# Moving one-off preparation of an attention and expert kernel ahead of its main loop, two score stacks prepared by transfers

## The chip, the cores and the metric

The kernel runs on one core of a Trainium2 chip. A core has a matrix engine (TensorE, PE in the profile; PEld is its weight load), a vector engine (VectorE, DVE), an activation engine (ScalarE, ACT), a general engine (GpSimd, POOL) and a synchronisation engine (SyncE, SP), which here issues every transfer. Each engine runs its own list of instructions in order, and waits on semaphores for the others. The metric is the time of one execution on the device in microseconds (us).

## The reference, cut to what matters

`x` is (32, 256, 128): 32 sequences of 256 tokens with 128 features. There are 16 heads of width 8 and 8 experts.

```python
def _attn(x, Wq, bq, Wk, bk, Wv, bv, Wo, bo):      # x: (b, s, 128)
    q, k, v = ((x @ W.T + c).reshape(b, s, 16, 8).transpose(0, 2, 1, 3) for W, c in ...)
    scores = jnp.einsum('bhqd,bhkd->bhqk', q, k) / math.sqrt(8)
    scores = jnp.where(causal, scores, -jnp.inf)
    out = jnp.einsum('bhqk,bhkd->bhqd', softmax(scores), v)
    return out.transpose(0, 2, 1, 3).reshape(b, s, 128) @ Wo.T + bo

def _experts(x, gate_w, We):
    top_val, top_idx = jax.lax.top_k(jnp.einsum('btd,ed->bte', x, gate_w), 2)
    y_all = jnp.einsum('btd,edm->btem', x, We)
    return (take(y_all, top_idx) * softmax(top_val)[..., None]).sum(axis=2)

xn = layernorm(x)
return x + _attn(xn, ...) + _experts(xn, ...)
```

## The kernel before

**One sequence is one unit of work, and 34 slots are laid over 32 sequences.** `over_slots` writes slot `s` for every engine. In slot `s` the kernel takes the scores of sequence `s` with queries as rows, only for their maxima (`score_item` on PE, `take_max` on DVE); the scores of sequence `s-1` with keys as rows, exponentials and weighted values (`scoreT_item`, `take_exp`, `values`), which run `LAG` = 4 items behind and so reach into slot `s+1`; the experts of sequence `s-1`; the output of sequence `s-2`; the projections of sequence `s+2` (`PRE`); and the normalisation of sequence `s+3` (`NXT`). A slot has twelve score items, and each engine's share of the other work stands at fixed item numbers `n`.

**The stacks.** The scores need q and k of a head as bf16 triples (high, middle and low part), stacked as rows of one contraction. `qstack` and `kstack` hold, for each of four buffers, 128 partitions by 16 heads by 256 tokens in bf16, that is 8 KB a partition. Rows 0 to 71 (to 79 for q, with zeros) are loaded for each sequence: ACT, DVE and POOL write the three parts (`part1`, `take_rest`, `part2`, `part3`) into `parts`, SP stores them to a DRAM scratch, waits for that, and loads them back in the order of the stack, six transfers a sequence (`stacks`). One or two more rows (from `MAX_ROW` = 72) take the maxima of `mT`, by two small transfers a sequence. Rows 80 to 122 (`MASK_ROW` to `ALL_ROWS`) of q, and 72 to 122 of k, are the same for all sequences: they encode the causal mask. They are made once in `q_steps` and `k_steps` by POOL and copied into the upper 64 partitions of each stack (`fill_stack` on DVE, `fill_keys` on ACT). `vaug` (values padded with zeros and ones) also needs a one-off fill of each of four buffers.

**What sets the order around the change.** Everything is written out by hand. Before slot 0 stands a preamble: input loads, three normalisations, two projections, the fill of three or four stacks. `between` does one-off work behind slots 0 to 3: on DVE `fill_vaug`, the fill of query stacks 2 and 3 and the split of the expert weights into two halves; on ACT the fill of key stacks 2 and 3 and its part of the split. SP's list in slot `s` is: store the output of sequence `s-3`, load the maxima `mT` of sequence `s-1`, load an input, then `stacks` for sequence `s+2`, whose loads wait in the first slots for `dve_stack` and `act_stack`. All transfers are on SP's one queue.

Of the kernel before, what the change touches and what calls it, by code (L numbers as in the profile page):

```python
# [27 lines left out]
ALU = mybir.AluOpType  # L28
# [86 lines left out]
def bass_block(nc, x, wq, wk, bq, bk, wv, bv, wo, bo, gate, we, out):  # L115
    ctx = ExitStack()
    with ctx:
# [12 lines left out]
        def sems(*names):  # L130
# [80 lines left out]
        act_stack, dve_stack, dve_fill, dve_zero, dve_weights, act_weights = sems(  # L211
            "act_stack", "dve_stack", "dve_fill", "dve_zero", "dve_weights", "act_weights")
# [5 lines left out]
        dve_stats, dve_mv, pool_eps, pool_rstd, pool_xn = sems("dve_stats", "dve_mv", "pool_eps", "pool_rstd", "pool_xn")  # L218
# [13 lines left out]
        LOOP0 = 4  # L232
# [4 lines left out]
        def over_slots(slot, between=None):  # L237

            for s in range(NSEQ + 2):
                slot(Seq(0, s), s)  # L240
                if between and s < LOOP0:
                    between(s)
# [14 lines left out]
        def _(sp):  # L257
# [22 lines left out]
            def stacks(pre, s):  # L280
# [17 lines left out]
                rows = scr.rearrange("a (d h) t -> (a d) (h t)", h=H)  # L298
                qs, ks = (st[pre.buf][:].rearrange("p h t -> p (h t)") for st in (qstack, kstack))
                sp.wait_ge(dma_scratch_q, upto(pre, unit=16))  # L300
                for r in range(PARTS):
                    n = PART_ROWS + (ZERO_ROWS if r == PARTS - 1 else 0)
                    sp.dma_start(qs[r * PART_ROWS:r * PART_ROWS + n], rows[0:n]).then_inc(dma_stack[pre.buf], 16)
                sp.wait_ge(dma_scratch_k, upto(pre, per=2, unit=16))
                for r in range(PARTS):
                    turned = PART_ROWS + ZERO_ROWS + r * HD
                    sp.dma_start(ks[r * PART_ROWS:(r + 1) * PART_ROWS],
                                 rows[turned:turned + PART_ROWS]).then_inc(dma_stack[pre.buf], 16)

            def slot(t, s):  # L310
# [8 lines left out]
                if has(s, NB):  # L319
                    new = t + NB  # L320
                    sp.wait_ge(pool_xn, upto(t))
                    sp.wait_ge(pool_xb, upto(t))
                    sp.dma_start(x_sb[new.buf][:], x_t[new.n]).then_inc(dma_x[new.buf], 16)
# [3 lines left out]
            for s in range(-PRE, 0):  # L327
                stacks(Seq(0, s + PRE), s)
            over_slots(slot)
# [5 lines left out]
        def _(pool):  # L335
            g = nc.gpsimd

            def normalise(nxt):
# [3 lines left out]
                pool.wait_ge(pool_eps, upto(nxt))  # L342
                g.tensor_tensor(rstd[:], var_eps[:], minus_half[:], ALU.pow).then_inc(pool_rstd, 1)  # L343
                pool.wait_ge(pool_rstd, upto(nxt))
# [5 lines left out]
                ins.then_inc(pool_xn, 1)  # L350
# [9 lines left out]
            def mask_steps():  # L360
                g.memset(q_steps[:], 0.0).then_inc(pool_const, 1)
                g.memset(k_steps[:], 0.0).then_inc(pool_const, 1)
                pool.wait_ge(pool_const, CONSTS)

                for i in range(STEPS):
                    g.affine_select(out=k_steps[:], in_=k_steps[:], compare_op=ALU.is_gt, fill=B_STEPS[i],
                                    base=1 + i - STEPS * MASK_ROW, pattern=[[-1, P]], channel_multiplier=STEPS).then_inc(pool_steps, 1)
                    pool.wait_ge(pool_steps, 2 * i + 1)
                    g.affine_select(out=q_steps[:], in_=q_steps[:], compare_op=ALU.not_equal, fill=A_STEPS[i],
                                    base=STEPS * MASK_ROW - i, pattern=[[1, P]], channel_multiplier=-STEPS).then_inc(pool_steps, 1)  # L370
                    pool.wait_ge(pool_steps, 2 * i + 2)
                g.affine_select(out=k_steps[:], in_=k_steps[:], compare_op=ALU.is_ge, fill=1.0,
                                base=-MASK_ROW, pattern=[[0, P]], channel_multiplier=1).then_inc(pool_steps, 1)
# [76 lines left out]
            normalise(Seq(0, 0))  # L450
            mask_steps()
            normalise(Seq(0, 1))
            part3(Seq(0, 0))
            normalise(Seq(0, 2))
            part3(Seq(0, 1))
            over_slots(slot)


        @block.scalar
        def _(act):  # L460
# [16 lines left out]
            def take_values(t, s):  # L477
# [4 lines left out]
                if s < NB:  # L482
                    act.wait_ge(dve_fill, 1 + s)
# [77 lines left out]
            def fill_keys(b):  # L561

                a.copy(kstack[b][HALF:P].rearrange("p h (q t) -> p (h q) t", q=QT),  # L563
                       k_steps[HALF:P].unsqueeze(1).to_broadcast([HALF, H * QT, P])).then_inc(act_stack, 1)
# [13 lines left out]
            copy_input(Seq(0, 0))  # L578
            round_input(Seq(0, 0))
            act.wait_ge(ld_bqk, 16 * 2)  # L580
            part1(Seq(0, 0))
            part2(Seq(0, 0))
            copy_input(Seq(0, 1))
            round_input(Seq(0, 1))
            part1(Seq(0, 1))
            part2(Seq(0, 1))
            copy_input(Seq(0, 2))
            round_input(Seq(0, 2))
            act.wait_ge(pool_steps, 2 * STEPS + 1)
            fill_keys(1)  # L590
            over_slots(slot, between)


        @block.vector
        def _(dve):
# [65 lines left out]
            def halve_input(nxt):  # L661
                dve.wait_ge(act_xnT, upto(nxt))
# [14 lines left out]
            def moments(nxt):  # L677
                dve.wait_ge(dve_stats, upto(nxt))
                dve.wait_ge(pool_xn, upto(nxt + (-1)))
# [12 lines left out]
            def slot(t, s):  # L692
                mix, fin = t + (-1), t + (-2)
                for n in range(ITEMS):
# [35 lines left out]
                    if n == 11 and has(s, NXT):  # L730
                        halve_input(t + NXT)
# [7 lines left out]
            def fill_vaug(b):  # L739

                v.memset(vaug[b][:], 0.0).then_inc(dve_zero, 1)
                dve.wait_ge(dve_zero, 2 + b)
                vv = vaug[b][:].rearrange("p q h c -> p (q h c)")
                ins = v.memset(bass.AP(tensor=vv.tensor, offset=vv.offset + HD,
                                       ap=[list(vv.ap[0]), [VGRP * VW, QT * H // VGRP], [VW + OW, VGRP]]), 1.0)
                ins.then_inc(dve_fill, 1)
# [5 lines left out]

            def between(s):
                if s < NB - 1:
                    fill_vaug(s + 1)
                if s < 2:
                    fill_stack(qstack[s + 2], q_steps)
                if s == 0:
                    dve.wait_ge(ld_we, 16)
                    dve.wait_ge(act_weights, 1)  # L760
                    high_half(we_sb[:], w_high[:]).then_inc(dve_weights, 1)
                    dve.wait_ge(dve_weights, 3)
                    low_half(we_sb[:], w_high[:], we_hl[:, 1]).then_inc(dve_weights, 1)
# [8 lines left out]
            halve_input(Seq(0, 0))  # L772
            measure(Seq(0, 1))
            moments(Seq(0, 1))
            dve.wait_ge(ld_w, 16 * NW)
            dve.wait_ge(dve_zero, 1)
            v.tensor_scalar(bv_wide[:], bv_wide[:], bv_sb[:], None, ALU.add).then_inc(dve_const, 1)
# [4 lines left out]
            halve_input(Seq(0, 1))  # L782
            dve.wait_ge(pool_const, CONSTS)
            dve.wait_ge(pool_steps, 2 * STEPS + 1)
            fill_stack(qstack[0], q_steps)
            fill_stack(kstack[0], k_steps)
            take_rest(Seq(0, 1))
            fill_stack(qstack[1], q_steps)
            dve.wait_ge(pe_bias, 1)
            dve.wait_ge(ld_bias, 16)  # L790
            v.tensor_tensor(bias_out[:], bias_out[:], m0[:, 0:D], ALU.add).then_inc(dve_bias, 1)
            fill_vaug(0)
            halve_input(Seq(0, 2))
            over_slots(slot, between)
# [3 lines left out]
        def _(pe):  # L798
# [9 lines left out]
            def score_item(t, n):  # L808
# [76 lines left out]
            def turn_input(nxt):  # L885
                pe.wait_ge(pool_xn, upto(nxt))
# [13 lines left out]
            def slot(t, s):  # L900
                pre, mix, fin = t + PRE, t + (-1), t + (-2)
                for n in range(ITEMS):
                    f, k = behind(t, s, n)
                    if has(s, 0):
                        score_item(t, n)
# [21 lines left out]
                    if n == 3 and has(s, -2):  # L927
# [16 lines left out]
                    if n == 6 and has(s, -2):  # L944
# [43 lines left out]
            project(Seq(0, 0))  # L988
            pe.wait_ge(dve_halves, 2)
            turn_input(Seq(0, 1))  # L990
            pe.wait_ge(ld_w, 16 * NW)
# [37 lines left out]
```

## Time and profile before

| | us |
|---|---|
| median of 3 runs (534.1 to 536.69) | 535.9 |
| the profiled execution, its own time | 535.46 |
| its span, first to last instruction | 533.7 |
| busy: PE / PEld / DVE | 484.4 / 397.5 / 420.5 |
| busy: ACT / POOL | 400.8 / 349.4 |

The profile is one execution. Sums below are made on the span, and 1.8 us (535.46 less 533.7) lie outside it. Its time is 0.4 us from the median, so a change of the span is read as the same change of the median.

### The profile page before, as it was taken

To read this page: it belongs to the slowest core of one execution; us is meant where nothing else is said; L and a number is where in the kernel's file an instruction comes from. 1 tells how busy PE (TensorE), PEld (TensorE's weight loads), DVE (VectorE), ACT (ScalarE), POOL (GpSimd) and SP (SyncE) were. 2 spreads that over 40 slices of the span, in tenths; PEclk is the share of its full clock that TensorE was granted. 3 is DMA by queue.
4 is the path that set the end of the run, shared out by engine and by line. 5 is a ranking of instruction groups with operands and counts; after the bars stand their busy time and mean duration, and the time that the engine had idled before them with its cause. 6 is when DMAs were issued, how large, how long until landed. Compare 5 with 4: busy or idle time off the path is not lost.

```text
span 533.7 us, 17265 instructions
## 1 busy us (share of the span) xinstructions
PE 484.4 (91%) x6274; PEld 397.5 (74%) x6274; DVE 420.5 (79%) x1108; ACT 400.8 (75%) x1063; POOL 349.4 (65%) x563
## 2 busy tenths in 40 slices
PE   1275678999999999999999999999999999999995
PEld 1153557788888888888888888888888888787863
DVE  3686466888888889888888888888988888887741
ACT  2525376787888888888888888888888888887774
POOL 6641345677777777777777777777777777864533
PEclk9975578999999999999999999999999999999999
DMA  4663345555566566665546565555666656553000
GB/s 123 163 153 67 78 104 146 125 143 139 133 143 145 134 143 152 150 152 149 144 117 167 127 154 140 143 134 142 147 155 155 151 133 156 127 123 72 14 12 22
DMA packets 64053, 67.79 MB, mean 127 GB/s; under 512 B 6752, under 2 KB 59104, under 8 KB 59104
## 3 DMA queue, kind: packets, MB, share of 16 engines
q1 hardware_dynamic: 63968, 66.68, 51.5%
q8 instruction: 50, 0.82, 0.7%
q14 instruction: 35, 0.29, 0.2%
HBM read 44.90 MB, written 21.23 MB: 124 GB/s over the span
## 4 chain that ended last, share of the span: by engine, by line
PE 77%; DMA 7%; ACT 5%; DVE 4%; issue 3%; SPq 2%; POOL 1%; POOLq 0%; DVEq 0%; ACTq 0%
PE m L805 19%; PE oT_ps L873 16%; PE scoreT_ps L849 10%; PE score_ps L829 10%; PE scoreT_ps L854 6%; DMA qstack<-mT 6%; PE score_ps L823 5%; PE m L956 3%; PE m L913 3%; PE m L974 2%; ACT upper L520 2%; PE m L888 2%; DVE negmax L606 1%; ACT kstack L563 1%; PE m L981 1%
## 5 line engine op out<-in xcount | busy, mean ns | idle before, releaser
L606 DVE TENSOR_REDUCE negmax<-score_ps 128x2 f32<-128x512 f32 (+1 forms) x384 | 249.9, 678 | 61.9 <-PE score_ps L829 57.0
L475 ACT ACTIVATE probs<-scoreT_ps 128x512 f32<-128x512 f32 x384 | 216.6, 603 | 85.5 <-PE scoreT_ps L854 44.8
L379 POOL TENSOR_TENSOR fours<-lower,upper 128x512 f32<-128x512 f32 x64 | 81.7, 1277 | 62.4 <-ACT upper L520 62.4
L805 PE MATMUL m<-we_hl,xnT_hl 128*128 128x512 f32 x384 | 115.6, 423 | 0.0
L849 PE MATMUL scoreT_ps<-qstack,kstack 123*128 123x128 bf16 (+1 forms) x1024 | 102.3, 222 | 12.1 <-DMA qstack<-mT 9.7
L829 PE MATMUL score_ps<-kstack,qstack 72*128 72x128 bf16 (+1 forms) x1024 | 104.3, 224 | 9.6 <-DVE negmax L606 9.3
L873 PE MATMUL oT_ps<-probs,vaug 128*32 128x256 f32 (+1 forms) x2048 | 99.1, 335 | 0.0
L849 PEld LDWEIGHTS scoreT_ps<-qstack,kstack 123*128 123x128 bf16 (+1 forms) x1024 | 70.1, 99 | 26.1 <-issue 20.4
L829 PEld LDWEIGHTS score_ps<-kstack,qstack 72*128 72x128 bf16 (+1 forms) x1024 | 72.6, 100 | 12.5 <-DVE negmax L606 11.9
L873 PEld LDWEIGHTS oT_ps<-probs,vaug 128*32 128x32 f32 x2048 | 58.3, 111 | 30.2 <-issue 2.2
L520 ACT ACTIVATE upper<-m,weight 128x128 f32<-128x128 f32 x256 | 73.1, 376 | 8.2 <-PE m L805 8.2
L805 PEld LDWEIGHTS m<-we_hl,xnT_hl 128*128 128x128 f32 x384 | 66.8, 194 | 8.8
L358 POOL TENSOR_TENSOR parts<-rest,parts 128x256 bf16<-128x256 f32 x64 | 42.7, 688 | 36.3 <-ACT parts L504 36.3
L823 PE MATMUL score_ps<-kstack,qstack 123*128 123x128 bf16 x512 | 51.6, 225 | 6.7 <-DMA kstack<-scratch 6.4
L348 POOL TENSOR_SCALAR xn<-x_sb,mv,rstd 128x128 f32<-128x128 f32 x64 | 51.5, 809 | 7.8 <-POOL rstd L343 7.8
L854 PE MATMUL scoreT_ps<-qstack,kstack 123*128 123x128 bf16 x512 | 51.3, 223 | 0.0
L854 PEld LDWEIGHTS scoreT_ps<-qstack,kstack 123*128 123x128 bf16 x512 | 30.8, 99 | 21.9 <-ACT probs L475 13.4
L643 DVE TENSOR_TENSOR lower<-m,weight 128x512 f32<-128x512 f32 x64 | 43.5, 679 | 3.2 <-PE m L805 3.2
L418 POOL TENSOR_TENSOR pairs<-fours 128x512 f32<-128x512 f32 x32 | 41.5, 1297 | 2.5
L823 PEld LDWEIGHTS score_ps<-kstack,qstack 123*128 123x128 bf16 x512 | 35.7, 100 | 8.0 <-issue 6.8
L805 PE MATMUL m<-xnT_hl,wqk_hl 128*128 128x256 f32 x192 | 33.5, 314 | 2.6 <-DVE xnT_hl L659 2.6
L689 DVE SCALAR_TENSOR_TENSOR rest<-m,bqk_sb,parts 128x256 f32<-128x256 f32 x64 | 28.0, 478 | 5.3 <-ACT parts L498 2.4
(79 smaller groups left out, 646.0 us busy)
## 6 DMA issues: line engine op xcount, KB each, us to landing
kstack<-scratch SPq DMA_DIRECT2D x96, 192.0 KB
scratch<-parts SPq DMA_DIRECT2D x64, 192.0 KB, 2.3
qstack<-scratch SPq DMA_DIRECT2D x64, 192.0 KB
qstack<-scratch SPq DMA_DIRECT2D x32, 256.0 KB
x_sb<-in_x SPq DMA_DIRECT2D x32, 128.0 KB, 2.3
scratch<-parts SPq DMA_DIRECT2D x32, 128.0 KB, 1.9
out<-out_sb SPq DMA_DIRECT2D x32, 128.0 KB, 3.6
qstack<-mT SPq DMA_DIRECT2D x64, 8.0 KB, 2.1
```

Of the source, the lines that this page charges most:

```text
L348: ins = g.tensor_scalar(xn[:, q, :], x_sb[nxt.buf][:, q, :], mv[:, q, 0:1], rstd[:, q:q + 1], ALU.subtract, ALU.mult)
L379: g.tensor_tensor(fours[:, :, q, :], lower[:, :, q, :], upper[:, :, q, :], ALU.add).then_inc(pool_sum, 1)
L475: a.activation(o, i, ACT.Exp, scale=SCALE).then_inc(act_exp, 1)
L520: ins = a.activation(upper[:, e, q, :], m2[:, e * D:(e + 1) * D], ACT.Copy, scale=weight[m.buf][:, q, EH + e:EH + e + 1])
L606: v.tensor_reduce(o, score_ps[n % 2][:].rearrange("p (h k) -> p h k", h=w), axis=AX.X, op=ALU.max, negate=True).then_inc(dve_max, 1)
L643: v.tensor_tensor(lower[:, :, q, :], m1[:].rearrange("p (e m) -> p e m", e=EH), weight[m.buf][:, q, 0:EH].unsqueeze(2).to_broadcast([P, EH ...
L805: ins = tn.matmul(o, l, r, start=first, stop=l is low)
L823: ins = tn.matmul(ps[:, c * P:(c + 1) * P], qs[0:ALL_ROWS, h, 0:P], ks[0:ALL_ROWS, h, 0:P], start=True, stop=True)
L829: ins = tn.matmul(ps[:, c * S + q * P:c * S + (q + 1) * P], qs[0:top, h, P:S], ks[0:top, h, q * P:(q + 1) * P], start=True, stop=True)
L849: ins = tn.matmul(ps[:, c * S + q * P:c * S + (q + 1) * P], ks[0:top, h, 0:P], qs[0:top, h, q * P:(q + 1) * P], start=True, stop=True)
L854: ins = tn.matmul(ps[:, c * P:(c + 1) * P], ks[0:ALL_ROWS, h, P:S], qs[0:ALL_ROWS, h, P:S], start=True, stop=True)
L873: ins = tn.matmul(o, va[:, q, h, :], i, start=q == 0 and grp % VGRP == 0, stop=q == 1 and grp % VGRP == VGRP - 1, skip_group_check=True)
```

## The change

Seven things are done, at the two ends of the program. The work of the slots between keeps its order; POOL gets one more wait in its normalisation.

1. The fills of `vaug` go from DVE (behind slots) to POOL (before slot 0), all four of them.
2. The mask rows are made earlier on POOL; stacks 0 and 1 are filled by DVE before slot 0; stacks 2 and 3 are filled by four transfers from stack 0, which SP issues behind the loads of sequence 1.
3. The expert weights are split before slot 0, on DVE and ACT.
4. The first three normalisations are done by DVE instead of POOL, which only prepares the factor (`spread`).
5. The six loads of the first stack become twelve, eight heads each; slot 0 starts on the first six.
6. ACT rounds before it copies in the preamble, and DVE waits there for PE instead of ACT.
7. In the last two slots the weighted values of the last sequence are taken at other items.

The core of the diff:

```diff
             def stacks(pre, s):
...
-                if s + PRE < NB:
-
-                    sp.wait_ge(dve_stack, s + PRE + 2)
-                    sp.wait_ge(act_stack, s + PRE)
+                if s < 0:
+                    sp.wait_ge(dve_stack, 2 * (s + PRE + 1))
                     sp.wait_ge(ld_zero, 16 * NB)
...
+                def load(heads, sem):
+                    sp.wait_ge(dma_scratch_q, upto(pre, unit=16))
+                    for r in range(PARTS):
+                        n = PART_ROWS + (ZERO_ROWS if r == PARTS - 1 else 0)
+                        sp.dma_start(qs[r * PART_ROWS:r * PART_ROWS + n, heads], rows[0:n, heads]).then_inc(sem, 16)
+                    sp.wait_ge(dma_scratch_k, upto(pre, per=2, unit=16))
+                    for r in range(PARTS):
...
+                if s == -PRE:
+                    load(slice(0, H // 2), dma_first)
+                    load(slice(H // 2, H), dma_stack[pre.buf])
+                else:
+                    load(slice(0, H), dma_stack[pre.buf])
...
             for s in range(-PRE, 0):
                 stacks(Seq(0, s + PRE), s)
+            for b in range(PRE, NB):
+
+                sp.dma_start(qstack[b][MASK_ROW:ALL_ROWS], qstack[0][MASK_ROW:ALL_ROWS]).then_inc(dma_fill[b], 16)
+                sp.dma_start(kstack[b][MAX_ROW:ALL_ROWS], kstack[0][MAX_ROW:ALL_ROWS]).then_inc(dma_fill[b], 16)
             over_slots(slot)
...
-            def normalise(nxt):
+            def spread(nxt):
                 pool.wait_ge(dve_mv, upto(nxt))
                 stand_alone(pool, pool_passed)
                 g.tensor_scalar(var_eps[:], mv[:, :, 1], 1.0, EPS, ALU.mult, ALU.add).then_inc(pool_eps, 1)
                 pool.wait_ge(pool_eps, upto(nxt))
+                pool.wait_ge(xn_done, upto(nxt + (-1)))
+                stand_alone(pool, pool_passed)
                 g.tensor_tensor(rstd[:], var_eps[:], minus_half[:], ALU.pow).then_inc(pool_rstd, 1)
...
+            mask_step(0)
+            mask_step(1)
+            spread(Seq(0, 0))
+            mask_step(2)
...
+            fill_vaug(0)
+            spread(Seq(0, 1))
+            fill_vaug(1)
             part3(Seq(0, 0))
-            normalise(Seq(0, 2))
+            spread(Seq(0, 2))
+            fill_vaug(2)
             part3(Seq(0, 1))
+            fill_vaug(3)
             over_slots(slot)
...
-            def between(s):
-                if s == 0:
-                    act.wait_ge(dve_weights, 3)
-                    a.copy(we_hl[:, 0], w_high[:]).then_inc(act_weights, 1)
-                if s < 2:
-                    fill_keys(s + 2)
...
+            for k in range(NXT):
+                round_input(Seq(0, k))
+                act.wait_ge(dve_halves, upto(Seq(0, k), per=2))
+                copy_input(Seq(0, k))
...
-            def between(s):
-                if s < NB - 1:
-                    fill_vaug(s + 1)
-                if s < 2:
-                    fill_stack(qstack[s + 2], q_steps)
-                if s == 0:
...
-                if n == 0:
+                if n == 0 and s == 0:
+                    pe.wait_ge(dma_first, 16 * NSTACK)
+                if n == (ITEMS // 2 if s == 0 else 0):
                     pe.wait_ge(dma_stack[t.buf], 16 * NSTACK * (t.turn + 1))
+                if n == 0 and PRE <= s < NB:
+                    pe.wait_ge(dma_fill[t.buf], 16 * 2)
...
-                    if n == 3 and has(s, -2):
+                    if s == NSEQ and n in (9, 11):
+                        values(mix, (9, 11).index(n))
+                    if s == NSEQ + 1 and n in (2, 4):
+                        values(fin, (2, 4).index(n) + 2)
+                    if n == 3 and has(s, -2) and s <= NSEQ:
```

**SP, from the loads of sequence 1 to those of sequence 2.** Each row is a line, what is written from what with the buffer's number, and the shape as partitions by elements. Before:

```order
L303 DMA qstack1<-scratch1 24x4096 x2
L303 DMA qstack1<-scratch1 32x4096
L307 DMA kstack1<-scratch1 24x4096 x3
L323 DMA x_sb0<-in_x 128x2x128
L285 DMA scratch2<-parts 128x2x256
L287 DMA scratch2<-parts 128x3x256
L289 DMA scratch2<-parts 128x3x256
L303 DMA qstack2<-scratch2 24x4096 x2
```

After:

```order
L302 DMA qstack1<-scratch1 24x4096 x2
L302 DMA qstack1<-scratch1 32x4096
L306 DMA kstack1<-scratch1 24x4096 x3
L336 DMA qstack2<-qstack0 43x4096
L337 DMA kstack2<-kstack0 51x4096
L336 DMA qstack3<-qstack0 43x4096
L337 DMA kstack3<-kstack0 51x4096
L328 DMA x_sb0<-in_x 128x2x128
L284 DMA scratch2<-parts 128x2x256
L286 DMA scratch2<-parts 128x3x256
L288 DMA scratch2<-parts 128x3x256
L302 DMA qstack2<-scratch2 24x4096 x2
```

Four transfers of 43 or 51 rows of 8 KB now stand between the loads of stack 1 and everything that follows on the queue.

**DVE, from the end of slot 0 to the first maximum of slot 1.** Before, with `between(0)` in the middle:

```order
L655 TENSOR_SCALAR xnT_high<-m1 128x256
L659 TENSOR_TENSOR xnT_hl3<-m1,xnT_high 128x256
L741 MEMSET vaug1 128x1024
L744 MEMSET vaug1 128x16x2
L750 COPY qstack2<-q_steps 64x4096
L655 TENSOR_SCALAR w_high<-we_sb 128x1024
L659 TENSOR_TENSOR we_hl<-we_sb,w_high 128x1024
```

After:

```order
L618 TENSOR_REDUCE negmax0<-score_ps1 128x2
L667 TENSOR_SCALAR xnT_high<-m1 128x256
L671 TENSOR_TENSOR xnT_hl3<-m1,xnT_high 128x256
L618 TENSOR_REDUCE negmax1<-score_ps0 128x4
L618 TENSOR_REDUCE negmax1<-score_ps1 128x2
```

Slot 1 follows slot 0 at once. The preamble's end has taken the work; after the change it reads:

```order
L704 SCALAR_TENSOR_TENSOR rest<-m2,bqk_sb,parts 128x256 x2
L765 COPY qstack1<-q_steps 64x4096
L765 COPY kstack1<-k_steps 64x4096
L667 TENSOR_SCALAR xnT_high<-m1 128x256
L671 TENSOR_TENSOR xnT_hl2<-m1,xnT_high 128x256
L799 TENSOR_TENSOR bias_out<-bias_out,m0 128x128
L667 TENSOR_SCALAR w_high<-we_sb 128x1024
L671 TENSOR_TENSOR we_hl<-we_sb,w_high 128x1024
L618 TENSOR_REDUCE negmax0<-score_ps0 128x4
```

The split of the expert weights and one more stack now stand ahead of the first maximum.

## Rows read from the trace of the kernel before

**Rows 1.** Stretches: us, busy of each engine (instructions), clock, transfer share, GB/s.

```profile
40.00:59.00 19.00, 7.68 (x35) 5.62 (x36) 9.10 (x23) 7.12 (x11) 4.20 (x8) 0.50 0.48 100
110.00:200.00 90.00, 89.73 (x1226) 74.70 (x1215) 78.36 (x216) 74.30 (x204) 65.68 (x106) 1.00 0.59 141
```

**Rows 2.** Timeline of DVE: the first maxima of slots 0 to 4.

```profile
27.46 1.29 DVE L606 TENSOR_REDUCE negmax<-score_ps 128x4 f32<-128x512 f32 x2 [4.39 <-PE score_ps L823]
...
44.09 1.28 DVE L606 TENSOR_REDUCE negmax<-score_ps 128x4 f32<-128x512 f32 x2
...
70.41 1.29 DVE L606 TENSOR_REDUCE negmax<-score_ps 128x4 f32<-128x512 f32 x2
...
92.69 0.66 DVE L606 TENSOR_REDUCE negmax<-score_ps 128x4 f32<-128x512 f32 x1
...
106.97 0.68 DVE L606 TENSOR_REDUCE negmax<-score_ps 128x4 f32<-128x512 f32 x1
```

**Rows 3.** The chain of work that ended last: start, length, what.

```profile
20.18 6.52 DMA kstack<-scratch
...
44.02 3.61 ACT kstack L563
...
50.72 7.66 DMA qstack<-mT
...
75.67 5.68 DMA qstack<-mT
```

**Rows 4.** Timeline of SP and PE: loads of stacks, maxima, second scores.

```profile
18.18 1.13 SPq L303 DMA_DIRECT2D qstack<-scratch  x3
...
28.49 1.19 SPq L307 DMA_DIRECT2D kstack<-scratch  x3
...
47.68 1.11 SPq L303 DMA_DIRECT2D qstack<-scratch  x3
...
50.07 1.24 SPq L318 DMA_DIRECT2D qstack<-mT  x2
...
58.52 0.58 PE L849 MATMUL scoreT_ps<-qstack,kstack 123*128 123x128 bf16 x4 [5.77 <-DMA qstack<-mT]
...
72.35 1.11 SPq L303 DMA_DIRECT2D qstack<-scratch  x3
```

**Rows 5.** Timeline of the preamble.

```profile
5.80 1.59 POOL L348 TENSOR_SCALAR xn<-x_sb,mv,rstd 128x128 f32<-128x128 f32 x2 [0.24 <-POOL rstd L343]
...
10.24 0.26 DVE L777 TENSOR_SCALAR bv_wide<-bv_wide,bv_sb 128x128 f32<-128x128 f32 x1
...
22.65 0.42 DVE L659 TENSOR_TENSOR xnT_hl<-m,xnT_high 128x256 fp32r<-128x256 f32 x1
```

**Rows 6.** Timeline of DVE around the fills behind slots 0 and 1.

```profile
39.84 0.91 DVE L741 MEMSET vaug<- 128x1024 f32 x1 [0.16 <-issue]
...
40.96 1.22 DVE L750 COPY qstack<-q_steps 64x4096 bf16<-64x4096 bf16 x1
...
42.95 1.23 DVE L659 TENSOR_TENSOR we_hl<-we_sb,w_high 128x1024 fp32r<-128x1024 f32 x1
...
66.99 0.42 DVE L659 TENSOR_TENSOR xnT_hl<-m,xnT_high 128x256 fp32r<-128x256 f32 x1
```

**Rows 7.** Stretches in the loads of one stack, in the steady part; columns as in rows 1.

```profile
131.30:131.60 0.30, 0.30 (x6) 0.30 (x4) 0.30 (x2) 0.30 (x2) 0.30 (x1) 1.00 0.71 300
...
133.00:135.00 2.00, 2.00 (x25) 1.85 (x23) 2.00 (x5) 1.63 (x4) 1.66 (x2) 1.00 0.71 164
```

**Rows 8.** Transfers, times from issue to landing: the tile `mT`, and the page.

```profile
DMA to landing us min/median/max: 1.8/2.1/7.8
...
scratch<-parts SPq DMA_DIRECT2D x64, 192.0 KB, 2.3
```

**Rows 9.** The chain in the last slot.

```profile
521.18 1.04 ACT upper L520 x4
...
527.13 0.59 ACT oT L538
```

More of the change, by code:

```diff
@@ L231, in bass_block, with over_slots @@
         NQK, NW, CONSTS = 2, 4, 8
-        LOOP0 = 4
         x_t = x.rearrange("(s q p) d -> s p q d", q=QT, p=P)
         out_t = out.rearrange("(s q p) d -> s p q d", q=QT, p=P)
-        def over_slots(slot, between=None):
+        def over_slots(slot):
             for s in range(NSEQ + 2):
                 slot(Seq(0, s), s)
-                if between and s < LOOP0:
-                    between(s)
         def has(s, k):
@@ L342, in normalise @@
                 pool.wait_ge(pool_eps, upto(nxt))
+                pool.wait_ge(xn_done, upto(nxt + (-1)))
+                stand_alone(pool, pool_passed)
                 g.tensor_tensor(rstd[:], var_eps[:], minus_half[:], ALU.pow).then_inc(pool_rstd, 1)
+            def normalise(nxt):
+                spread(nxt)
                 pool.wait_ge(pool_rstd, upto(nxt))
@@ L358, in part3, with mask_step, fill_vaug @@
                     g.tensor_tensor(parts[:, c, 2, :], rest[:, c, :], parts[:, c, 1, :], ALU.subtract).then_inc(pool_part3, 1)
[L360 to L373, printed above, removed]
+            def mask_step(i):
+                g.affine_select(out=k_steps[:], in_=k_steps[:], compare_op=ALU.is_gt, fill=B_STEPS[i],
+                                base=1 + i - STEPS * MASK_ROW, pattern=[[-1, P]], channel_multiplier=STEPS).then_inc(pool_steps, 1)
+                pool.wait_ge(pool_steps, 2 * i + 1)
+                g.affine_select(out=q_steps[:], in_=q_steps[:], compare_op=ALU.not_equal, fill=A_STEPS[i],
+                                base=STEPS * MASK_ROW - i, pattern=[[1, P]], channel_multiplier=-STEPS).then_inc(pool_steps, 1)
+                pool.wait_ge(pool_steps, 2 * i + 2)
+            def fill_vaug(b):
+                g.memset(vaug[b][:], 0.0).then_inc(pool_zero, 1)
+                pool.wait_ge(pool_zero, 1 + b)
+                vv = vaug[b][:].rearrange("p q h c -> p (q h c)")
+                ins = g.memset(bass.AP(tensor=vv.tensor, offset=vv.offset + HD,
+                                       ap=[list(vv.ap[0]), [VGRP * VW, QT * H // VGRP], [VW + OW, VGRP]]), 1.0)
+                ins.then_inc(pool_fill, 1)
             def sum_tile(m, q):
@@ L577, in _ @@
             a.copy(wqk_hl[:, 0], w_high[:, 0:2]).then_inc(act_weights, 1)
[L578 to L591, printed above, removed]
+            for k in range(NXT):
+                round_input(Seq(0, k))
+                act.wait_ge(dve_halves, upto(Seq(0, k), per=2))
+                copy_input(Seq(0, k))
+                if k == 0:
+                    act.wait_ge(ld_bqk, 16 * 2)
+                if k < PRE:
+                    part1(Seq(0, k))
+                    part2(Seq(0, k))
+            act.wait_ge(dve_weights, 3)
+            a.copy(we_hl[:, 0], w_high[:]).then_inc(act_weights, 1)
+            over_slots(slot)
         @block.vector
@@ L737, in slot, with first_normalised @@
                                         res[:].rearrange("p q d -> p (q d)"), ALU.add).then_inc(dve_out, 1)
[L739 to L746, printed above, removed]
+            def first_normalised(nxt):
+                dve.wait_ge(pool_rstd, upto(nxt))
+                dve.wait_ge(pe_xnT, upto(nxt + (-1)))
+                stand_alone(dve, dve_passed)
+                for q in range(QT):
+                    ins = v.tensor_scalar(xn[:, q, :], x_sb[nxt.buf][:, q, :], mv[:, q, 0:1], rstd[:, q:q + 1],
+                                          ALU.subtract, ALU.mult)
+                ins.then_inc(xn_done, 1)
             def fill_stack(stack, steps):
@@ L943, in slot @@
                         experts(mix, 1)
-                    if n == 6 and has(s, -2):
+                    if n == 6 and has(s, -2) and s <= NSEQ:
                         values(fin, 2)
```

102 lines of the change are left out of this document (53 added, 49 removed).

## The prediction, made before the changed kernel ran

> **What bounds the kernel now.** I read the stretches first. From 110 to 200 us PE is busy 89.73 of 90 us at the full clock (2.4 GHz) [rows 1], and the last two first maxima shown are 14.3 us apart, which is a slot [rows 2]; the change leaves these slots as they are. The loss is at the start: from 40 to 59 us PE works 7.68 of 19 us, at a granted clock of 0.50 (1.2 GHz) [rows 1]. Slots 0 to 2 take 16.6, 26.3 and 22.3 us where slot 3 takes 14.3 [rows 2]. About 22 us are lost there, and 27 pass before slot 0.
>
> The chain says on what. Slot 0 waits for the loads of stack 0 until 26.7 us. ACT's 3.6 us fill of a key stack holds back the loads of stack 2; behind these on SP's list stand the two small `mT` transfers of sequence 0. They land 7.7 us after their issue, and only then do the second scores begin, at 58.52. The same comes again in slot 2, where an `mT` transfer holds the chain for 5.7 us [rows 3, 4]. `mT` takes 2.1 us in the median and 7.8 at most [rows 8]: issued right behind six loads, it waits for them. So **the queue is first in, first out**, and what stands ahead of `mT` sets the start of the second scores.
>
> **The preamble and slot 0.** Two normalisations cost POOL 1.59 us; a DVE operation of that shape took 0.26, so two are about 0.5 there, 1.1 us less for the first sequence, and as much again before the third step of the list [rows 5]. DVE's list before slot 0 ended at 23.07 [rows 5]. It gains one stack (1.2 us) and the expert halves (2.0, from 42.18 to 44.18), and loses a fill of `vaug` (1.0) [rows 6]. With 1.5 us of the normalisations' gain the first maximum comes at 23.07 + 1.2 + 2.0 - 1.0 - 1.5 = 23.8, or 3.7 us early. The loads do not hold it: six loads took from 18.2 to 26.7 [rows 3, 4], half the bytes take about 5.4, and issued two us earlier they land near 21.5; the second half is there by item 6, where PE now waits for it. Slot 0 takes 12.4 us, and the 4.2 of `between(0)` from 39.84 on are gone [rows 2, 6]: slot 1 would open near 36 instead of 44.09. POOL's four fills of `vaug` (0.9 each on DVE) I cost at nothing: the first is needed in slot 0, and one fill ahead of `part3`, 1 us late at worst, falls into a stretch that the next term swallows. The same goes for the new waits in the preamble.
>
> **The fills by transfer.** This term decides. SP issues four transfers of 43, 51, 43 and 51 rows of 8 KB behind the loads of stack 1. Those were all issued at 29.7 [rows 4]; stack 0's landed 6 us after their last issue, so stack 1's land near 36, and, all being some 1.5 us earlier, the fills begin to move at about 34.5. How fast? A stack is five transfers of 24 rows and one of 32. In their middle 0.71 of the 16 transfer engines are busy, about 12, though several such transfers are queued at a time [rows 7]. So 24 rows go to 12 engines, two each, and to the same 12 each time: if each transfer took others, the queue behind would keep all 16 busy. In every transfer of this kernel the shares can be equal (24 over 12; 32, 128 or 16 over 16). 43 is prime, and 51 is 3 times 17. **If shares must be equal, 43 rows go to one engine and 51 to three, 17 each.** If they need not be, 43 go three to an engine and 51 four. The trace fits both; equal shares are all that it has ever shown, and I take them.
>
> A rule of the Trainium skill speaks to this, and against the change: the page "DMA: Bandwidth & Descriptors", section "Why a DMA increments its semaphore by 16 and not by 1", has a transfer run on the largest number of engines, up to 16, that divides its slowest dimension, the lowest-numbered ones on SP's queue, and gives 127 partitions on one engine as an example. By it 24 rows take 12 engines, which the trace bears out, and the fills one and three, with the sum below; without it the sum would be the first rival's.
>
> The first engine then moves 43 + 17 + 43 + 17 = 120 rows. At 300 GB/s on 0.71 of 16 engines, the start of a load, an engine does 26 GB/s and a row 0.31 us; on the plateau, at 164 GB/s, where all write the same few partitions at once, a row takes 0.57 us (0.60 if 12 engines share it) [rows 7]. A lone engine has nothing beside it, so I take the first: **37.2 us**. The upper bound is 72.
>
> All that follows needs that engine too. The input of sequence 4 and the stores of sequence 2 have 128 partitions and so use every engine; queued on the first, they land at 34.5 + 37.2 + 2.2 = 73.9 us (an idle queue takes 2.3 [rows 8]). SP waits for these stores before it issues the loads of stack 2, and `mT` of sequence 0 stands behind those. From the first of these loads to the second scores it was 58.52 - 47.68 = 10.8 us in slot 1, and 81.35 - 72.35 = 9.0 in slot 2 [rows 3, 4]; with 10 they start at 83.9. Before, it was 58.52: **25.4 us later**. DVE waits too, for the input of sequence 4, behind which its part of `mT` stands, and ACT for the stores, but both go on at 75 and are not last. PE's new wait for the fills in slot 2 finds them long landed. The 8 us gained at slot 1 are swallowed whole.
>
> **What comes back.** Slot 2 opened 11.9 us after the second scores began, of which 3.0, from 67.41 to 70.41, were DVE's fills [rows 2, 4, 6]: **3.0 us** less. Slot 2 took 22.3; without ACT's second fill, and with stack 3 landed near 93, before slot 2 issues its `mT`, it takes what slot 3 takes, 14.3: **8.0 us** less. From slot 3 on nothing differs: POOL's added wait is for its own last normalisation, long done.
>
> **The last slots.** Two of four value groups go from slot 33 to slot 32, 1.4 us of PE. There they stand ahead of the experts' last products, for which ACT works from 521.18 in the chain; the final copy begins at 527.13 [rows 9]. PE's end gets shorter and ACT's chain longer: **0.5 us** less, between 0 and 1.4.
>
> **Sum.** 25.4 - 3.0 - 8.0 - 0.5 = 13.9 us more, on the profiled execution's 535.46: 549.4. That time is 0.4 from the median. As 0.31 us a row is the lower bound, I say 550.
>
> **Rivals.**
> *Uneven shares (faster).* 43 rows over 15 engines and 51 over 13: the busiest moves 14 rows, 4.3 us at 0.31 and 8.4 at 0.60. With 8 the stores land at 44.7, the second scores start at 54.7, 3.8 us early instead of 25.4 late, and the sum is -3.8 - 3.0 - 8.0 - 0.5 = -15.3: 520, and 516 at the lower price. For it: the trace fits. Against: no uneven share has been seen. It decides once the fills hold the queue for less than 37.2 - 13.9 = 23 us. Chance 0.11.
> *Equal shares, each transfer on other engines (faster).* The two of 43 rows run side by side, 13.3 us; stores at 50.0, second scores at 60.0, sum -10: 525. The plateau at 0.71 speaks against it. Chance 0.04.
> *A dearer row (slower still).* No bulk transfer within the core's memory is in the trace. At 0.45 us a row the fills take 54 and the time is 566; at 0.60 it is 584. For it: the plateau. Against: rows with few others beside them take 0.31. Chance of over 0.45: 0.09.
> *The fills cost nothing and the change does all it can.* Slot 0 at 23.8, slots of 12.4, 14.3 and 14.3, slot 3 near 65 instead of 92.69: 507. Even spread evenly the rows need 4.3 us. Chance 0.02.
>
> **Numbers.** One engine at 0.31 to 0.45 us a row has 0.71, with its own range of 546 to 566; above it 0.09; the faster cases 0.17; between them, within 0.5% of no change (about what a measurement of this kernel can tell), 0.03. The range goes from 543 to 575: it leaves out the faster cases and some 3 in 100 above.
>
> **What would show it.** Right: PE, DVE and ACT all but idle in slot 1 from about 38 to 73 us, at the low clock; a transfer share near 1/16 and some 26 GB/s there, three times that for 5 us twice; the second scores near 84, slot 2 near 93, slot 3 near 107, and slots of 14.3 from there. Wrong: a share over 0.7 after 34 us and slot 3 before 85. If the share is near 1/16 and the stretch longer, the price of a row was wrong.

## The result, and the profile after

The changed kernel takes 551.7 us (median of 4 runs, 548.77 to 553.78) against 535.76 us before (4 runs): the ratio is 1.0297, with an interval of 1.0243 to 1.0351. It is slower by 3.0%, close to the 550 that was forecast. The profiled execution has a span of 549.0 us, 15.3 more than before. One execution of 700.59 us, in the run with 46 rows below, with a granted clock of 0.67, is left out of its median and ratio.

The page of the changed kernel, its span, busy times, granted clock and transfers (40 slices of 13.7 us):

```profile
span 549.0 us, 17301 instructions
PE 479.5 (87%) x6274; PEld 394.6 (72%) x6274; DVE 417.5 (76%) x1105; ACT 390.1 (71%) x1060; POOL 348.6 (63%) x565
PE   2560039999999999999999999999999999999995
DVE  6860028888888878888888888988888888887721
PEclk9965559999999999999999999999999999999997
GB/s 120 193 112 56 53 146 110 147 147 147 150 145 155 122 169 114 156 140 137 149 130 151 134 155 138 142 143 150 149 153 129 163 123 161 130 127 59 14 13 20
```

No engine works more than before; all are empty in the fourth and fifth slice, where the transfers move 53 to 56 GB/s. The timeline of DVE gives the first maximum of slots 0 to 4 and of slot 31, which answer to [rows 2]:

```profile
24.97 0.68 DVE L618 TENSOR_REDUCE negmax<-score_ps 128x4 f32<-128x512 f32 x1
...
35.54 0.68 DVE L618 TENSOR_REDUCE negmax<-score_ps 128x4 f32<-128x512 f32 x1
...
89.00 0.68 DVE L618 TENSOR_REDUCE negmax<-score_ps 128x4 f32<-128x512 f32 x1
...
103.50 0.68 DVE L618 TENSOR_REDUCE negmax<-score_ps 128x4 f32<-128x512 f32 x1
...
118.29 0.68 DVE L618 TENSOR_REDUCE negmax<-score_ps 128x4 f32<-128x512 f32 x1
...
509.45 0.69 DVE L618 TENSOR_REDUCE negmax<-score_ps 128x4 f32<-128x512 f32 x1
```

Slots 0 and 1 open 2.5 and 8.6 us early. Then slot 1 takes 53.5 us, and slot 3 opens 10.8 us late (103.50 against 92.69). What SP does meanwhile, from the last loads of stack 1 to the second scores' `mT` (its own timeline; the second number is how long the issue of the transfer took):

```profile
26.23 1.19 SPq L306 DMA_DIRECT2D kstack<-scratch  x3
27.46 0.73 SPq L336 DMA_DIRECT2D qstack<-qstack  x1
28.23 0.72 SPq L337 DMA_DIRECT2D kstack<-kstack  x1
29.00 0.60 SPq L336 DMA_DIRECT2D qstack<-qstack  x1
29.64 0.69 SPq L337 DMA_DIRECT2D kstack<-kstack  x1
30.44 17.25 SPq L328 DMA_DIRECT2D x_sb<-in_x  x1
47.80 4.57 SPq L284 DMA_DIRECT2D scratch<-parts  x1
52.43 4.91 SPq L286 DMA_DIRECT2D scratch<-parts  x1
57.39 7.08 SPq L288 DMA_DIRECT2D scratch<-parts  x1
71.96 1.13 SPq L302 DMA_DIRECT2D qstack<-scratch  x3
...
74.36 1.22 SPq L323 DMA_DIRECT2D qstack<-mT  x2
```

The four fills are issued in 2.9 us. The input load behind them cannot even be issued for 17 us, and the loads of stack 2, which waited for the stores, come at 71.96; they came at 47.68 before [rows 4]. The stretches show what the transfer engines do in that time (columns as in [rows 1]):

```profile
40.00:44.00 4.00, 0.00 (x0) 0.00 (x0) 0.00 (x0) 0.00 (x0) 0.00 (x0) 0.50 0.19 78
44.00:48.00 4.00, 0.00 (x0) 0.00 (x0) 0.00 (x0) 0.00 (x0) 0.00 (x0) 0.50 0.07 29
...
56.00:60.00 4.00, 0.00 (x0) 0.00 (x0) 0.00 (x0) 0.00 (x0) 0.00 (x0) 0.50 0.23 73
60.00:64.00 4.00, 0.00 (x0) 0.00 (x0) 0.00 (x0) 0.00 (x0) 0.00 (x0) 0.50 0.06 25
```

From 60 to 64 us the share is 0.06, one engine of sixteen, at 25 GB/s; from 40 to 44 it is 0.19, three engines, at 78. (From 48 on the input and the stores behind the fills are issued, which would be what raises the share to 0.23 from 56 to 60; the view does not say whose bytes they are.) The waiters are read in the timeline: DVE for the input of sequence 4, ACT for the stores, PE for `mT`:

```profile
71.26 0.48 DVE L689 BATCH_NORM_STATS2 stats<-x_sb 128x6 f32<-128x128 f32 x2 [34.44 <-DMA x_sb<-in_x]
72.56 0.84 ACT L525 ACTIVATE parts<-m,bqk_sb 128x256 bf16<-128x256 f32 x2 [34.79 <-DMA scratch<-parts]
81.29 0.59 PE L864 MATMUL scoreT_ps<-qstack,kstack 123*128 123x128 bf16 x4 [5.28 <-DMA qstack<-mT]
```

That is what the forecast looked for: one engine busy, all else idle, and the queue let go at 71. Two things remain to be told apart: whether it is the number of engines that a row count allows, and not the bytes or the kind of transfer; and whether the queue or the engine is held.

### The profile page after: what moved, and what is told of

The parts are those of the page before. It is cut to its first block, busy times and chain, and to the rows that moved or that the text cites. A ratio compares the mean times of both kernels' runs of the same rounds, so it can differ in the third digit from the quotient of the medians.

```text
span 549.0 us, 17301 instructions
## 1 busy us (share of the span) xinstructions
PE 479.5 (87%) x6274; PEld 394.6 (72%) x6274; DVE 417.5 (76%) x1105; ACT 390.1 (71%) x1060; POOL 348.6 (63%) x565
## 4 chain that ended last, share of the span: by engine, by line
PE 75%; DMA 9%; SPq 4%; ACT 4%; issue 3%; POOL 3%; DVE 1%; POOLq 0%; ACTq 0%; DVEq 0%
PE m L816 18%; PE oT_ps L888 15%; PE scoreT_ps L864 10%; PE score_ps L844 10%; PE scoreT_ps L869 6%; PE score_ps L838 5%; DMA qstack<-mT 4%; DMA scratch<-parts 4%; PE m L975 3%; SPq L328 3%; PE m L928 2%; PE m L993 2%; ACT upper L547 2%; ACT probs L502 1%; PE m L903 1%
## 5 line engine op out<-in xcount | busy, mean ns | idle before, releaser
L816 PE MATMUL m<-we_hl,xnT_hl 128*128 128x512 f32 x384 | 114.4, 420 | 0.0
L888 PE MATMUL oT_ps<-probs,vaug 128*32 128x256 f32 (+1 forms) x2048 | 96.9, 329 | 1.3 <-ACT probs L502 1.2
L888 PEld LDWEIGHTS oT_ps<-probs,vaug 128*32 128x32 f32 x2048 | 57.2, 109 | 30.4 <-ACT probs L502 1.9
L816 PEld LDWEIGHTS m<-we_hl,xnT_hl 128*128 128x128 f32 x384 | 65.7, 192 | 9.3 <-issue 0.4
L525 ACT ACTIVATE parts<-m,bqk_sb 128x256 bf16<-128x256 f32 x64 | 26.7, 472 | 39.0 <-DMA scratch<-parts 36.7
L362 POOL TENSOR_SCALAR xn<-x_sb,mv,rstd 128x128 f32<-128x128 f32 x58 | 46.1, 801 | 7.0 <-POOL rstd L354 7.0
L689 DVE BATCH_NORM_STATS2 stats<-x_sb 128x6 f32<-128x128 f32 x64 | 15.3, 280 | 36.6 <-DMA x_sb<-in_x 36.6
L402 POOL TENSOR_TENSOR gap<-top 128x2 f32<-128x2 f32 x32 | 6.3, 196 | 55.6 <-DVE top L627 55.5
```

The source lines that it names most:

```text
L362: ins = g.tensor_scalar(xn[:, q, :], x_sb[nxt.buf][:, q, :], mv[:, q, 0:1], rstd[:, q:q + 1], ALU.subtract, ALU.mult)
L816: ins = tn.matmul(o, l, r, start=first, stop=l is low)
L888: ins = tn.matmul(o, va[:, q, h, :], i, start=q == 0 and grp % VGRP == 0, stop=q == 1 and grp % VGRP == VGRP - 1, skip_group_check=True)
```

## The experiments

"Slot 2 opens" below is DVE's first maximum of slot 2 in each run's profile: 70.41 us before, 89.00 after the change. A run's median is over its own executions; its ratio and interval are against the kernel before, on the same chip.

### Row counts that can be shared equally

The fills run on to partition 127, which is filled already in the source; five more rows each.

```diff
-                sp.dma_start(qstack[b][MASK_ROW:ALL_ROWS], qstack[0][MASK_ROW:ALL_ROWS]).then_inc(dma_fill[b], 16)
-                sp.dma_start(kstack[b][MAX_ROW:ALL_ROWS], kstack[0][MAX_ROW:ALL_ROWS]).then_inc(dma_fill[b], 16)
+                sp.dma_start(qstack[b][MASK_ROW:P], qstack[0][MASK_ROW:P]).then_inc(dma_fill[b], 16)
+                sp.dma_start(kstack[b][MAX_ROW:P], kstack[0][MAX_ROW:P]).then_inc(dma_fill[b], 16)
```

> The four fill transfers take 48 and 56 rows instead of 43 and 51 (up to partition 127), so that equal shares exist on 16 and 14 engines: more bytes, 3 + 4 + 3 + 4 = 14 rows on the busiest engine instead of 120. Theory 'equal shares and one queue': the fills hold the queue 4 to 8 us instead of 37.4, the second scores of sequence 0 start near 52 us instead of 81.3, and the time is 551.7 - 29 = 523 (519 to 527). Rival 'the transfers are dear by their bytes or by their kind, memory to memory of the core': no faster than the change as it stands, 550 to 556.

Measured: 524.3 us, ratio 0.9817 (0.9782 to 0.9853). Slot 2 opens at 63.32.

With 11% more bytes in the fills the kernel is 27 us faster than the change, and 1.8% faster than before. Bytes and kind of transfer are excluded as the cause of those 27 us. The fills are not cheap all the same: the second scores start at 55.61, where 52 was expected. A stretch of this run in slot 1:

```profile
36.00:40.00 4.00, 3.30 (x20) 2.86 (x19) 0.78 (x2) 0.79 (x4) 0.00 (x0) 1.00 0.91 143
```

At 143 GB/s on 0.91 of 16 engines an engine does 9.8 GB/s, and a row takes 0.83 us, more than the 0.60 that [rows 7] gave as the upper bound. This is an estimate: the input and the stores move in the same stretch, and the stretch before it (32 to 36 us, 178 GB/s on all engines) gives 0.75.

### Only the k fills stay at 51 rows

```diff
-                sp.dma_start(qstack[b][MASK_ROW:ALL_ROWS], qstack[0][MASK_ROW:ALL_ROWS]).then_inc(dma_fill[b], 16)
+                sp.dma_start(qstack[b][MASK_ROW:P], qstack[0][MASK_ROW:P]).then_inc(dma_fill[b], 16)
```

> Only the q fills take 48 rows; the k fills keep their 51 rows. Theory 'equal shares': 3 + 17 + 3 + 17 = 40 rows of 0.31 us on the busiest engine, 12.5 us, second scores near 57 us, time near 528 (524 to 532), that is 4 to 6 us above the run with 48 and 56 rows. Rival 'uneven shares are possible and something else was slow': same as the run with 48 and 56 rows.

Measured: 532.07 us, ratio 0.9938 (0.9915 to 0.9961), just over the range that was expected, and 7.8 us above the run with 48 and 56 rows where 4 to 6 were; slot 2 opens at 69.72. It lies between the two, as three engines of 17 rows should, and from 48 to 52 us the share is 0.19, three engines.

### 46 rows, even but twice a prime

```diff
-                sp.dma_start(qstack[b][MASK_ROW:ALL_ROWS], qstack[0][MASK_ROW:ALL_ROWS]).then_inc(dma_fill[b], 16)
-                sp.dma_start(kstack[b][MAX_ROW:ALL_ROWS], kstack[0][MAX_ROW:ALL_ROWS]).then_inc(dma_fill[b], 16)
+                sp.dma_start(qstack[b][MASK_ROW:P - 2], qstack[0][MASK_ROW:P - 2]).then_inc(dma_fill[b], 16)
+                sp.dma_start(kstack[b][MAX_ROW:P], kstack[0][MAX_ROW:P]).then_inc(dma_fill[b], 16)
```

> The q fills take 46 rows (2 times 23), the k fills 56. Theory 'largest number of engines up to 16 that divides the rows': 46 rows go to two engines, 23 rows each, 7.2 us instead of some 2 for 48 rows, twice, so 8 to 11 us more than the run with 48 and 56 rows: 532 to 536. Rival 'only odd or prime counts are slow, or rows are dealt out unevenly': 523 to 526.

Measured: 536.17 us, the median of nine executions (ratio 1.0021, 0.9998 to 1.0043), 12 us over the run with 48 rows, for two rows fewer, where 8 to 11 were expected; slot 2 opens at 73.77. While PE stands still the share falls to two engines of sixteen, at 53 GB/s:

```profile
44.00:48.00 4.00, 0.00 (x0) 0.00 (x0) 0.00 (x0) 0.00 (x0) 0.00 (x0) 0.50 0.13 53
```

So one, two and three engines are seen for 43, 46 and 51 rows. The number of engines is a divisor of the rows, and neither parity nor an uneven deal explains it. Powers of two alone do not either: 51 rows would then have had one engine, and 24 rows eight, where [rows 7] have 0.71 of sixteen busy.

The four runs can be put on one line by SP's first load of stack 2, which waits for the queue: 46.05, 52.73, 55.63 and 71.96 us with 48 and 56 rows, 48 and 51, 46 and 56, 43 and 51. Take 0.83 us for a row of a transfer on 14 or 16 engines, and 0.31 on one to three. The busiest engine is then held for 14 x 0.83 = 11.6, for 6 x 0.83 + 34 x 0.31 = 15.5, for 8 x 0.83 + 46 x 0.31 = 20.9 and for 120 x 0.31 = 37.2 us. The differences are 34.4, 37.2, 34.7 and 34.8: three agree, and the second is 2.5 us off, which I can't explain. The holds are estimates; with 0.75 in place of 0.83 the four differences lie between 34.8 and 37.7.

### The same fills from ACT's own queue

The four transfers of 43 and 51 rows are taken out of SP's list and put at the end of ACT's preamble.

```diff
+            act.wait_ge(dve_stack, 2)
+            for b in range(PRE, NB):
+
+                a.dma_start(qstack[b][MASK_ROW:ALL_ROWS], qstack[0][MASK_ROW:ALL_ROWS]).then_inc(dma_fill[b], 16)
+                a.dma_start(kstack[b][MAX_ROW:ALL_ROWS], kstack[0][MAX_ROW:ALL_ROWS]).then_inc(dma_fill[b], 16)
             act.wait_ge(dve_weights, 3)
```

> The four fills keep 43 and 51 rows but are issued by ACT on its own queue, at the end of its preamble, about 22 us. Theory 'first in, first out in one queue': the stores and loads of SP's queue pass the fills, slot 1 goes on without a gap, and only slot 2 waits for the fill of stack 2 (18.7 us of one engine, from 22 us on, so about 42 to 50): time 520 to 530. Rival 'the engine is the bottleneck, whatever the queue': the first engine alternates between the two queues, the small pieces of the stores each wait for a row of 8 KB, and the second scores still start only at 70 to 80 us: time 540 to 552.

Measured: 548.16 us, ratio 1.0272 (1.0234 to 1.031). The timeline of ACT's queue and of the waits behind it:

```profile
22.52 1.20 ACTq L600 DMA_DIRECT2D qstack<-qstack  x1
23.75 0.73 ACTq L601 DMA_DIRECT2D kstack<-kstack  x1
24.51 1.34 ACTq L600 DMA_DIRECT2D qstack<-qstack  x1
25.89 15.70 ACTq L601 DMA_DIRECT2D kstack<-kstack  x1
```

```profile
45.25 0.38 SPq L284 DMA_DIRECT2D scratch<-parts  x1
45.68 1.57 SPq L286 DMA_DIRECT2D scratch<-parts  x1
47.30 0.48 SPq L288 DMA_DIRECT2D scratch<-parts  x1
62.46 1.11 SPq L302 DMA_DIRECT2D qstack<-scratch  x3
71.49 1.10 SPq L306 DMA_DIRECT2D kstack<-scratch  x3
```

The issue of the last fill holds ACT for 15.7 us, so this run has a delay of its own: ACT is late for the first values. But the stores, issued from 45.25 to 47.8 on a queue that holds none of the fills, let the q loads go only at 62.46 and the k loads only at 71.49, while an idle queue took 2.3 us for such a store [rows 8]. The order on SP's queue can't be the reason. A queue of its own does not help: **the engine is held, not the queue**. Whether the engine alternates between the two queues in these 24 us, or first works off rows that it had already taken, stays open.

### The last values where they were

On the run with 48 and 56 rows, the two slots at the end are put back:

```diff
-                    if s == NSEQ and n in (9, 11):
-                        values(mix, (9, 11).index(n))
-                    if s == NSEQ + 1 and n in (2, 4):
-                        values(fin, (2, 4).index(n) + 2)
-                    if n == 3 and has(s, -2) and s <= NSEQ:
+                    if n == 3 and has(s, -2):
...
-                    if n == 6 and has(s, -2) and s <= NSEQ:
+                    if n == 6 and has(s, -2):
```

> As the run with 48 and 56 rows, and the values of the last two slots are taken where the kernel before takes them. The tail from slot 31 to the end was 39.6 us after the change and 37.1 before, by the two profiles. Theory 'the values moved to slot 32 lengthen ACT's chain': 2 to 3 us less than the run with 48 and 56 rows. Rival (the prediction's own term): 0.5 us more.

Measured: 522.57 us, ratio 0.9785 (0.9744 to 0.9826); the medians are 1.7 us apart, and the intervals of the two runs overlap, so the times alone decide nothing. The other way round, the kernel before with these lines alone moved:

```diff
+                    if s == NSEQ and n in (9, 11):
+                        values(mix, (9, 11).index(n))
+                    if s == NSEQ + 1 and n in (2, 4):
+                        values(fin, (2, 4).index(n) + 2)
-                    if n == 3 and has(s, -2):
+                    if n == 3 and has(s, -2) and s <= NSEQ:
```

> The kernel before with only the values of the last two slots moved. Theory 'they lengthen ACT's chain': 1 to 2.5 us slower than before, 0.2 to 0.5 per cent. Rival, the term of the prediction: 0.5 us faster, not to be told from no change.

Measured: 537.61 us, ratio 1.0056 (1.0033 to 1.0078): slower by 0.6%. From the first maximum of slot 31 to the end the profiles of these two pairs give 38.6 us with the lines (534.4 - 495.84 here, 522.2 - 483.63 in the run with 48 and 56 rows), and 37.0 to 37.1 without (520.6 - 483.57, and 533.7 - 496.63 before). The other profiles with the lines give 39.1 to 39.7, and the rest without them 37.1 to 37.7. The chain of the run with 48 and 56 rows shows where the 1.5 us are:

```profile
505.81 0.79 PE oT_ps L888 x16
506.60 0.89 PE m L816 x3
...
508.42 0.86 PE oT_ps L888 x16
509.27 0.91 PE m L816 x3
510.21 0.92 ACT upper L547 x4
511.22 1.11 ACT probs L502 x2
512.38 0.86 PE oT_ps L888 x16
```

Both value groups stand ahead of an expert product, and ACT's `upper`, behind which the last exponentials queue, waits for the second. The same chain in the run with the old tail has two products and no values before `upper`:

```profile
505.74 0.75 PE m L816 x3
...
508.12 1.04 ACT upper L547 x4
```

Counted from the first maximum of slot 31, `upper` starts at 26.6 us in the first and at 24.6 in the second, and ACT's last exponentials end at 31.1 and 29.5. In both the last copy of the weighted values (`oT`) starts 0.98 us after these. PE's shorter list gains nothing, because it waits for ACT.

### No transfers: DVE fills all stacks ahead of slot 0

```diff
-            for b in range(PRE, NB):
-
-                sp.dma_start(qstack[b][MASK_ROW:ALL_ROWS], ...).then_inc(dma_fill[b], 16)
-                sp.dma_start(kstack[b][MAX_ROW:ALL_ROWS], ...).then_inc(dma_fill[b], 16)
...
             fill_stack(kstack[1], k_steps)
+            for b in range(PRE, NB):
+                fill_stack(qstack[b], q_steps)
+                fill_stack(kstack[b], k_steps)
```

It has the old tail too.

> No fill transfers: DVE fills all four pairs of stacks ahead of slot 0 (four more copies of 1.2 us), and the last values are where the kernel before takes them. Theory 'what is lost in slot 1 is the queue held by the fills': slot 0 opens near 30 us instead of 25, but the second scores come 10 us after slot 1 opens at the latest, slot 2 opens near 54 to 57 us (63.3 with 48 and 56 rows), time 513 to 517. Rival 'copies on DVE cost as much as they free': 522 or more.

Measured: 515.75 us, ratio 0.9656 (0.9624 to 0.9688). The first maxima of slots 0 to 2:

```profile
30.61 0.68 DVE L613 TENSOR_REDUCE negmax<-score_ps 128x4 f32<-128x512 f32 x1
...
41.10 0.68 DVE L613 TENSOR_REDUCE negmax<-score_ps 128x4 f32<-128x512 f32 x1
...
54.49 0.68 DVE L613 TENSOR_REDUCE negmax<-score_ps 128x4 f32<-128x512 f32 x1
```

Slot 0 pays 5.6 us for four copies, and slot 1 shrinks to 13.4: from the start of slot 0 to the end of slot 2 no transfer stands in the chain.

### Transfers, but issued behind `mT`

48 and 56 rows, old tail, and the fills of stack 2 and 3 stand in slots 1 and 2 behind the `mT` transfers.

```diff
+                if PRE <= s + 1 < NB:
+                    b = s + 1
+                    sp.dma_start(qstack[b][MASK_ROW:P], qstack[0][MASK_ROW:P]).then_inc(dma_fill[b], 16)
+                    sp.dma_start(kstack[b][MAX_ROW:P], kstack[0][MAX_ROW:P]).then_inc(dma_fill[b], 16)
                 if has(s, NB):
                     new = t + NB
```

> Transfers of 48 and 56 rows, but issued where they hold up nothing: those for stack 2 behind the mT transfers of slot 1, those for stack 3 behind those of slot 2; last values as before the change. Theory 'only what stands ahead of mT on the queue costs': the second scores start near 46 us, slot 2 opens near 53, time 511 to 515. Rival 'the bytes cost wherever they stand': 519 to 524, as the run with early fills and the old tail.

Measured: 518.6 us, ratio 0.9707 (0.9676 to 0.9739). Slot 2 opens at 53.53, as expected, but the time lies 3.6 us over the range of the theory, and just under that of the rival. The later `mT` transfers now wait, 4.4 and 4.7 us of the chain in slots 2 and 3:

```profile
38.86 6.78 DMA qstack<-mT
...
56.96 4.39 DMA qstack<-mT
...
72.91 4.72 DMA qstack<-mT
```

The fills no longer stand ahead of the first `mT`, but they hold back the stores behind them, and so the loads of the next stack. These end 2.6 us before `mT` is issued, in slot 2 and in slot 3; in the run in which DVE fills the stacks they end 4.8 and 4.4 us before it, and only the second waits in the chain, for 3.3 us. So the place of the fills is worth 4.0 us (522.57 to 518.6), and the transfers still cost 2.9 us more than DVE's copies (515.75).

### Two key stacks by ACT

As the run with DVE's fills, but ACT fills key stacks 2 and 3 at the end of its preamble.

```diff
+            act.wait_ge(pool_steps, 2 * STEPS + 1)
+            for b in range(PRE, NB):
+                a.copy(kstack[b][HALF:P].rearrange("p h (q t) -> p (h q) t", q=QT),
+                       k_steps[HALF:P].unsqueeze(1).to_broadcast([HALF, H * QT, P])).then_inc(act_stack, 1)
             act.wait_ge(dve_weights, 3)
...
                 fill_stack(qstack[b], q_steps)
-                fill_stack(kstack[b], k_steps)
```

> As the run in which DVE fills all stacks ahead of slot 0, but the two key stacks 2 and 3 are filled by ACT at the end of its preamble (3.6 us each by the trace before), where it has nothing else to do before slot 0. Theory 'DVE's list sets the start of slot 0': two copies of 1.2 us less on DVE, slot 0 opens near 28.2 instead of 30.6 us, time 2.4 us less than that run: 513 (511 to 515). Rival 'the two engines slow each other, or ACT is late for the first values': 516 or more.

Measured: 515.54 us, ratio 0.9651 (0.9594 to 0.9708), the same as with DVE alone. Slot 0 opens at 28.38, 2.2 us earlier, as expected; ACT's copies end late, and DVE then waits 4.06 us for the first values:

```profile
26.42 7.11 ACT L600 COPY kstack<-k_steps 64x4096 bf16<-64x4096 bf16 x2
...
35.18 0.24 DVE L628 MAX8 top<-logits 128x8 f32<-128x8 f32 x2 [4.06 <-ACT vaug L514]
```

The gain at slot 0 is given back in it: slot 1 opens at 43.84, after 41.10 with DVE alone. ACT is late for the first values, as the rival said.

## Why the prediction was right

**The fills by transfer: right in mechanism and size.** One engine for 43 rows and three for 51 are shown by the share of 0.06 and 0.19, and by the runs with 48, 46 and 51 rows, where the rival of uneven shares would have given one time. The rule of the Trainium skill (page "DMA: Bandwidth & Descriptors", section "Why a DMA increments its semaphore by 16 and not by 1") agrees with the shares at 43, 46 and 51 rows. At 48 and 56 rows the share of 0.91 and more fits it, but does not tell 16 engines from 14. A row on a lone engine costs what the prediction took: the input behind the fills lands at about 71.2 against a fill end of 71.7 in the forecast, and the loads of stack 2 come at 71.96 against some 74. The second scores start at 81.29, where 83.9 was said: 22.8 us late instead of 25.4. The forecast added an idle queue's 2.2 us to the end of the fills, and that was too much by about as much; that the other fifteen shares had landed long before would explain it, but no view shows it. The sign "three times that for 5 us twice" did not come: 0.18 to 0.21 of the engines were busy in one stretch, from 33 to 44 us, and one engine alone after it. So the second and third engine did not wait for the first between the two fills of 51 rows; the sum needs the first engine alone and is not touched by it.

**The preamble: right, but without weight**, as forecast. First maximum at 24.97 (23.8 said), slot 1 at 35.54 (36): slot 0 opened 1.2 us later than said and was 1.8 shorter, and the two errors nearly cancel. What each part of the new preamble is worth was not tested alone.

**What comes back: a little more than said.** Slot 2 opened 7.7 us after the second scores, 4.2 less than before instead of 3.0. Slot 2 took 14.5, 7.8 less instead of 8.0. Slot 3 opened 10.8 us late; by the terms of the prediction it was 14.4.

**The steady slots: said unchanged, and 2.0 us longer in this profile.** From slot 3 to slot 31 it is 405.95 us, before 403.94. From slot 4 on it is 391.2 against 389.7, and the other runs, with the same steady code, lie between 389.1 and 392.7, so these 1.5 us are no more than the spread of the executions. The other 0.5 us are slot 3, and belong to the change: it takes 14.8 us against 14.3 (14.0 in the other profile with the old preamble), and 14.7 to 15.1 in every run with the new one but the late fills, which take 16.3. Why is not shown.

**The last slots: the term that failed, in sign.** "I take 0.5 us less" should have been 1.5 more. The prediction named both effects, 1.4 us less of PE and a longer chain on ACT, and let PE win without a price for ACT. ACT's chain decides, since PE waits for its last exponentials in either case. In the profile of the change the tail is 2.5 us longer. The part over 1.5 goes with the granted clock of the last ten microseconds, which was 0.67 here and 0.95 before, with PE busy for 8.4 and 8.7 of the ten before them:

```profile
539.00:549.00 10.00, 4.29 (x38) 2.58 (x34) 1.21 (x3) 2.04 (x4) 2.38 (x3) 0.67 0.05 15
```

With the lines moved the six profiles give 38.6 us at 0.90 (twice), 39.1 at 0.79 and 0.80, 39.6 at 0.67 and 39.7 at 0.65; without them 37.0 to 37.1 at 0.86 to 0.95, and 37.7 at 0.76.

The sum of 13.9 against 15.3 measured is therefore closer than its terms, and part of that is luck: 3.6 us too much at the start, 2.0 and 3.0 too little behind it.

**Queue or engine.** The prediction had the later transfers wait for the first engine, and gave the order of the one queue as the reason. The run on ACT's queue shows that it is the engine that all transfers share. For the kernel as changed the two give the same time; for a remedy they do not.

## What to carry to other kernels

Look at the row count of every transfer before its bytes: 43 rows of 8 KB on one engine, 13.3 us at 0.31 a row, cost more than a whole stack of 152 rows, whose six loads took 8.5 us from the first issue to the landing before the change. Going on to 48 and 56 rows turned a loss of 3.0% into a gain of 1.8%. A one-off transfer is not free because nobody waits for it; ask which engines it holds and what small, urgent transfer must pass through the same ones. Work that is moved in a program's last slots helps only if it leaves the chain: here it was put ahead of an experts' product for which ACT waits, and cost 1.5 us.

## What the runs showed of the hardware

- With over 100 rows of 8 KB given to one transfer engine, the issuer of the next transfer was held too: SP took 17.25 us to issue one load, and ACT 15.7 us to issue one fill, in which it did nothing else. With 14 such rows on the busiest engine the longest issue took 3.3 us, and in the first three slots of the kernel before an issue took 0.3 to 0.8 us.
- A row of 8 KB within the core's memory cost 0.31 us when one to three engines moved such rows, and an estimated 0.75 to 0.83 us when 14 to 16 did (178 and 143 GB/s in all, other transfers among them). From DRAM the same row cost 0.57 us with 12 engines [rows 7].
- Spreading the fills over 14 to 16 engines instead of one and three thus shortened them from 37 to about 12 us, by the same estimate, and not to a sixteenth.
- Transfers on another queue do not pass a held engine: stores on SP's queue took about 17 and 24 us while the fills stood on ACT's.
